# Layer norms in an attention part: statistics by batch-norm instructions on VectorE, normalising on ScalarE

## What is computed

```python
def _layernorm(x, axis=-1, eps=1e-05):
    m = jnp.mean(x, axis=axis, keepdims=True)
    v = jnp.var(x, axis=axis, keepdims=True)
    return (x - m) / jnp.sqrt(v + eps)
...
h = _L0_tok_ref(x, ...)                      # the tower
h = h + _L0_attn_ref(_layernorm(h), W_Q, W_K, W_V)
h = h + _L0_ffn_ref(_layernorm(h), ...)      # top 6 of 64 experts, softmax, projection, own norm
```

## Time and profile before

| what | us |
|---|---|
| median of the runs | 1521.6 |
| the profiled execution | 1521.73 |
| its span in the trace | 1520.0 |
| TensorE busy | 1371.7 |
| VectorE busy | 1183.7 |
| ScalarE busy | 532.2 |
| the attention part up to the experts | 1254 to 1344 |
| the experts and the last norms | 1344 to 1520 |

### The profile page before, as it was taken

How to read it: one execution, slowest core, us unless ns; L and a number is a source line. 1 busy time by engine, 2 the same in 40 slices (tenths; PEclk the granted TensorE clock), 3 DMA queues, 4 the chain that set the end, 5 groups by cost and what they waited for, 6 DMA issues and landing times. The chain is left out here.

```text
span 1520.0 us, 68982 instructions
## 1 busy us (share of the span) xinstructions
PE 1371.7 (90%) x32216; PEld 699.5 (46%) x32216; DVE 1183.7 (78%) x1451; ACT 532.2 (35%) x673; POOL 92.4 (6%) x45
## 2 busy tenths in 40 slices
PE   9889989998899999989999998888789999889996
PEld 3444444445444444454444445555531128843332
DVE  3489999997999999879999997665511118967886
ACT  2522222222222222132222223343379994511211
POOL 1000000000000000000000000000000000045551
PEclk9999999999999999999999999999999999989998
DMA  6233343336766666566666664688844521065420
GB/s 232 90 142 141 131 152 120 135 131 212 277 243 254 246 251 249 195 241 250 257 244 256 243 257 148 252 326 318 342 175 159 181 70 60 8 151 134 118 77 15
DMA packets 55614, 284.35 MB, mean 187 GB/s; under 512 B 16224, under 2 KB 18208, under 8 KB 25504
## 3 DMA queue, kind: packets, MB, share of 16 engines
q1 hardware_dynamic: 34352, 162.22, 32.0%
q10 hardware_dynamic: 21104, 119.76, 19.3%
HBM read 160.33 MB, written 121.63 MB: 186 GB/s over the span
## 5 line engine op out<-in xcount | busy, mean ns | idle before, releaser
L951 ACT ACTIVATE act_c<-slots,conv_b 128x1024 f32<-128x1024 f32 x234 | 258.7, 1115 | 657.4 <-PE slots L603 657.2
L826 DVE STREAM_TRANSPOSE inv_out<-slots 128x1024 f32<-128x1024 f32 x256 | 304.8, 1229 | 77.3 <-PE slots L565 77.3
L603 PEld LDWEIGHTS slots<-inv_w,inv_out 64*64 64x64 f32 x16384 | 268.7, 135 | 194.8 <-issue 184.4
L603 PE MATMUL slots<-inv_w,inv_out 64*64 64x64 f32 x16384 | 299.3, 223 | 14.5 <-issue 8.8
L802 DVE STREAM_TRANSPOSE turned_h<-slots 128x1024 f32<-128x1024 f32 x200 | 237.6, 1227 | 23.7 <-PE slots L498 23.6
L498 PE MATMUL slots<-turned_w,fwd_w 32*64 32x512 f32 x3200 | 204.8, 608 | 22.5 <-DVE inv_out L826 17.2
L777 DVE STREAM_TRANSPOSE turned_w<-act_c 128x1024 f32<-128x1024 f32 x186 | 219.7, 1223 | 0.0
L565 PE MATMUL slots<-turned_k,inv_h 64*64 64x320 f32 x2048 | 167.1, 439 | 36.4 <-DVE turned_h L802 24.4
L587 PE MATMUL slots<-xin,conv_w 32*32 32x512 f32 x3072 | 112.8, 604 | 29.3 <-DMA xin<-act_scratch 15.0
L510 PE MATMUL slots<-turned_h,fwd_h 64*64 64x320 f32 x1600 | 132.8, 443 | 2.1 <-DVE turned_h L802 1.3
L565 PEld LDWEIGHTS slots<-turned_k,inv_h 64*64 64x64 f32 x2048 | 68.1, 132 | 116.3 <-DVE turned_h L802 71.5
(11 more groups left out here) (179 smaller groups left out, 1173.8 us busy)
## 6 DMA issues: line engine op xcount, KB each, us to landing
act_scratch<-act_c ACTq DMA_DIRECT2D x113, 1024.0 KB, 4.1
xin<-act_scratch SPq DMA_DIRECT2D x96, 1024.0 KB, 4.9
act_c<-act_scratch SPq DMA_DIRECT2D x17, 1024.0 KB, 4.9
mode_w<-in_sw_dram SPq DMA_DIRECT2D x20, 640.0 KB, 4.6
at_turned<-level_scratch SPq DMA_DIRECT2D x24, 256.0 KB, 4.1
at_ret_t<-level_scratch SPq DMA_DIRECT2D x20, 256.0 KB, 4.2
xin<-in_x_dram SPq DMA_DIRECT2D x4, 1024.0 KB, 8.6
turned_w<-in_x_turned_dram SPq DMA_DIRECT2D x3, 1024.0 KB, 4.9
```

The lines of the kernel that those rows point to most:

```text
L603: mm = nc.tensor.matmul(banks[half * 64:(half + 1) * 64, 2 * two + odd, at:at + 64], inv_out[rows, t % 2, i, two, s, 2 * half:2 * half + 2 ...
L826: nc.vector.transpose(dst, src).then_inc(inv_turned, 1)
L951: nc.scalar.activation(home[:, :, at, :].rearrange("p i q m -> p q i m"), banks[:, at, :].rearrange("p q (i m) -> p q i m", i=2), ACT.Gelu ...
```

## The change

The norm of x for chunk 3 and all four norms of y are made in another way. Chunks 0 to 2 of x, and the norm of the result at the end, stay.

- `measure_last_x` and `measure_y` replace `centre_x(3)` and `centre_y`, at the same places of VectorE's list. `moments` takes 8 batch-norm statistics (one of each tile of 64 columns), 8 aggregations of them, and one instruction of 8 columns which makes a quarter of variance plus eps.
- `root` on ScalarE stays, on a quarter of the value.
- `scale_last_x` and `scale_y` replace `norm_x(3)` and `norm_y` on VectorE: `scale_and_shift` has five instructions of 8 columns, which give per tile a scale (the inverse root) and a shift (minus mean times the inverse root). The multiplication over 512 columns is gone from VectorE.
- `norm_last_x` and a new `norm_y` on ScalarE make the normalised tiles straight from h, with one activation per tile (8 for a chunk) that takes its scale and its shift from SBUF, one value per partition. For y each reads 64 columns and writes 128, both copies. `double_y` is gone.
- `norm_last_x` stands ahead of `move_x(3)` in ScalarE's list, and `norm_y(0)` behind it, where `double_y(0)` stood ahead. `norm_y(1)` to `norm_y(3)` stand where `double_y` stood.
- `y_turn` waits for `y_set` alone, which ScalarE now raises. `measure_y` of chunks 2 and 3 waits also for `norm_y` of the chunk two earlier, since the statistics lie in two buffers.

```diff
+def moments(nc, link, parts, src, stats):
+
+    for t in range(CT):
+        last = nc.vector.bn_stats(out=parts[:, t, :], in_=src[:, t, :])
+    link(last)
+    for t in range(CT):
+        last = nc.vector.bn_aggr(out=pairs_of(stats)[:, t, :], in_=parts[:, t, :])
+    link(last)
+    return nc.vector.tensor_scalar(stats[:, 1, :], pairs_of(stats)[:, :, 1], EPS, 0.25, ALU.add, ALU.mult)
+
+
+def pairs_of(stats):
+
+    return stats[:, 3:5, :].rearrange("p a t -> p (a t)").rearrange("p (t a) -> p t a", a=2)
+
+
+def scale_and_shift(nc, link, stats):
+
+    link(nc.vector.reciprocal(stats[:, 0, :], stats[:, 2, :]))
+    link(nc.vector.tensor_tensor(stats[:, 0, :], stats[:, 0, :], stats[:, 1, :], ALU.mult))
+    link(nc.vector.tensor_tensor(stats[:, 0, :], stats[:, 0, :], stats[:, 2, :], ALU.add))
+    link(nc.vector.reciprocal(stats[:, 2, :], stats[:, 0, :]))
+    return nc.vector.scalar_tensor_tensor(stats[:, 5, :], pairs_of(stats)[:, :, 0], -1.0, stats[:, 2, :],
+                                          ALU.mult, ALU.mult)
...
                 pe.wait_ge(y_set, c + 1)
-                pe.wait_ge(y_copied, c + 1)
                 turn(s, 128, lambda j: flat(y2[:, c * CT + j, :, :]))
...
-            def centre_x(c):
-
-                dve.wait_ge(h_in[c], 32)
-                centre(nc, link, h[:, tiles_of(c)], centred_x[:, c], squares[:, 0],
-                       stats_x[:, c]).then_inc(x_variance, 1)
...
+            def measure_last_x():
+
+                c = CHUNKS - 1
+                dve.wait_ge(h_in[c], 32)
+                moments(nc, link, parts, h[:, tiles_of(c)], stats_last).then_inc(x_variance, 1)
+
+            def scale_last_x():
+
+                dve.wait_ge(x_root, CHUNKS)
+                scale_and_shift(nc, link, stats_last).then_inc(x_scaled, 1)
...
-            def centre_y(c):
+            def measure_y(c):
 
                 wait_moved("attend", c)
-                centre(nc, link, h[:, tiles_of(c)], centred_y[:, c % 2], squares[:, 1],
-                       stats_y[:, c % 2]).then_inc(y_variance, 1)
-
-            def norm_y(c):
+                if c >= 2:
+                    dve.wait_ge(y_set, c - 1)
+                moments(nc, link, parts, h[:, tiles_of(c)], stats_y[:, c % 2]).then_inc(y_variance, 1)
+
+            def scale_y(c):
 
                 dve.wait_ge(y_root, c + 1)
-                invert_root(nc, link, stats_y[:, c % 2])
-                nc.vector.tensor_tensor(y2[:, tiles_of(c), 0, :], centred_y[:, c % 2],
-                                        along(stats_y[:, c % 2, 2], D), ALU.mult).then_inc(y_set, 1)
+                scale_and_shift(nc, link, stats_y[:, c % 2]).then_inc(y_scaled, 1)
...
             rotate(1, 1)
-            centre_x(3)
+            measure_last_x()
             decay_scores(0)
-            norm_x(3)
+            scale_last_x()
             add_heads(0)
-            centre_y(0)
+            measure_y(0)
             decay_scores(1)
-            norm_y(0)
+            scale_y(0)
             cross(2)
             rotate(2, 0)
             add_heads(1)
-            centre_y(1)
+            measure_y(1)
...
-            norm_y(1)
+            scale_y(1)
             decay_scores(3)
-            centre_y(2)
+            measure_y(2)
             add_heads(3)
-            centre_y(3)
-            norm_y(2)
+            measure_y(3)
+            scale_y(2)
             rank(1)
             take(1)
-            norm_y(3)
+            scale_y(3)
...
-            def double_y(c):
-
-                act.wait_ge(y_set, c + 1)
-                nc.scalar.copy(y2[:, tiles_of(c), 1, :], y2[:, tiles_of(c), 0, :]).then_inc(y_copied, 1)
+            def norm_last_x():
+
+                c = CHUNKS - 1
+                act.wait_ge(x_scaled, 1)
+                for t in range(CT):
+                    last = nc.scalar.activation(normed[:, c, t, :], h[:, c * CT + t, :], ACT.Identity,
+                                                scale=stats_last[:, 2, t:t + 1], bias=stats_last[:, 5, t:t + 1])
+                last.then_inc(normed_set, 1)
+
+            def norm_y(c):
+
+                act.wait_ge(y_scaled, c + 1)
+                for t in range(CT):
+                    last = nc.scalar.activation(y2[:, c * CT + t, :, :], across(h[:, c * CT + t, :], 2), ACT.Identity,
+                                                scale=stats_y[:, c % 2, 2, t:t + 1],
+                                                bias=stats_y[:, c % 2, 5, t:t + 1])
+                last.then_inc(y_set, 1)
...
             root_y(0)
             move_qkv(2, 1)
-            double_y(0)
+            norm_last_x()
             move_x(3)
+            norm_y(0)
             move_y(0)
...
-            double_y(1)
+            norm_y(1)
             move_y(1)
             root_y(2)
             move_gate(1)
             root_y(3)
-            double_y(2)
+            norm_y(2)
             move_y(2)
             exponent(1)
             move_gate(2)
-            double_y(3)
+            norm_y(3)
             move_y(3)
```

More of the change, by code:

```diff
@@ L1082, in transformer @@
         squares = sb("at_squares", [128, 3, CT, D])
-        stats_y = sb("at_stats_y", [128, 2, 3, CT])
+        stats_y = sb("at_stats_y", [128, 2, 6, CT])
+        stats_last = sb("at_stats_last", [128, 6, CT])
+        parts = sb("at_parts", [128, CT, 6])
         normed_t = sb("at_normed_t", [D, 2, SLOT])
@@ L1132, in transformer @@
         y_set = sem("ex_y_set")
-        y_copied = sem("ex_y_copied")
+        x_scaled = sem("at_x_scaled")
+        y_scaled = sem("ex_y_scaled")
         shifted = sem("ex_shifted")
@@ L1681, in root_x @@
                 act.wait_ge(x_variance, c + 1)
-                root(nc, stats_x[:, c]).then_inc(x_root, 1)
+                root(nc, stats_x[:, c] if c < CHUNKS - 1 else stats_last).then_inc(x_root, 1)
             def move_x(c):
```

## The result

The changed kernel takes 1530.4 us (median of 6 runs, 1527.97 to 1535.93); the kernel before, run beside it, takes 1522.38. The ratio is 1.0064 (95% interval 1.004 to 1.0088): the changed kernel is slower, by a little, and the interval leaves out 1. In a second comparison, with more runs of the kernel before, the ratio was 1.0103 (1.008 to 1.0126).

What follows compares the result with a forecast made beforehand. VectorE looked busiest, but late ScalarE norms would delay TensorE's transposes: 7.0 us of waiting plus 1.7 of clock make 8.7, giving 1530.4 from the profiled 1521.73, or 1530.3 against the median. Range: 1526.0 to 1533.0 us.

Steps and rivals of the forecast that it cites:

- 7.0 of waiting: Attention part: late norms on ScalarE delay y's transposes, and from softmax(2) on everything runs 7.0 us later.
- 1.7 of clock: Behind TensorE's wait ahead of y_turn(0): half clock for 3.4 us costs 1.7 us, bounds 0 and about 2.5.
- The walk: Step-by-step delays through the attention part: y_turn(0) 4.8 us late, cross(3) 3.5, y_turn(3) 8.0, the end 7.0.
- chain of waits around 1290 us: Attention part, 10 us from 1290: VectorE busy 9.55 us, the chain nearly VectorE alone, favouring taking work off it.
- VectorE's saving: Five norms in the attention part: 2.0 us saved per chunk, 10 us in all.
- ScalarE's prices: Activations with scale and shift from SBUF: 426 and 480 ns each; norm_last_x 2.8 us, norm_y 3.2 us.
- Rival (b): At y_turn(3): a second clock fall costs up to 1.5 us, with slower aggregations 0.3 more: 1532; chance 0.25.
- (a): ScalarE's activations: both operands fetched together, 334 ns; end 3.1 us late, 1524.7, or 1526.4 with clock fall; chance 0.13.
- (c): Attention part: no fall of the clock at all, 1528.6 us; chance 0.07.
- (d): At cross(3): VectorE's own list releases it, so all ten us saved reach the end, 1511.6; chance 0.02.
- (e): At measure_y(3): its new wait for norm_y(1) could bind, but costs nothing over the walk; no chance given.

Runs made afterwards that it cites:

- filled_waits: The changed kernel with dummy matmuls put into TensorE's waits ahead of x_turn(3) and y_turn(0) to y_turn(3): 1526.51 us, ratio 1.004 to the kernel before.
- fill_first: The changed kernel with dummy matmuls only ahead of x_turn(3) and y_turn(0): 1526.28 us, ratio 1.0044 to the kernel before.
- late_old: The changed kernel with y chunks 1 to 3 normalised the old way, x chunk 3 and y chunk 0 the new way: 1527.63 us, ratio 1.0058.
- one_operand: The changed kernel with activations taking only the scale from SBUF (shift left out) and dummies in TensorE's waits: 1520.43 us, ratio 1.0011 to before.

## Why the prediction was right, and where it was not

The sum was 7.0 of waiting and 1.7 of clock, thus 8.7; 8.0 was measured beside it. The walk was right and the clock was not: its term was 1.7 us and measured 6.9 to 9.6. That the total still fits the first comparison is luck, as the points below on the clock and on the profile of before show.

**The chain of before.** The prediction says that the chain of waits around 1290 us consists nearly of VectorE alone. It doesn't. From 1284.17 to 1294.25 it runs over TensorE and ScalarE (start and length, kernel before):

```profile
1286.17 0.89 PE slots L1228 x8
...
1287.08 1.02 ACT at_normed_t L1677
...
1288.23 1.54 PE slots L1249 x8
1289.77 1.02 PE slots L1228 x8
1290.79 1.49 PE slots L1249 x8
1292.28 1.97 PE slots L1292 x16
```

This is `x_turn(3)`, its move, and the list behind `y_turn(0)`, the very place into which the change put ScalarE's two rows of eight; VectorE has the chain again from 1294.28 to 1327. So the question with which the prediction begins, who sets the pace, had a different answer at the place that mattered. The sum doesn't suffer, since its walk goes through this place all the same.

**VectorE's saving.** Eight statistics take 1.11 us (forecast 1.10) and eight aggregations 0.64 (0.7). The saving of 10 us is there, 8.5 of it as busy time, and none of it reaches the end.

**ScalarE's prices.** 428 and 484 ns (forecast 426 and 480), rows of eight in 2.76 and 3.19 us (2.8 and 3.2). The rule of the Trainium skill for pointer operands, "ScalarE: Activation LUTs", section "What ACT_TABLE_LOAD costs", is borne out with 89 to 91 ns for the second one. The rule on small tiles, of the Trainium skill's page "VectorE: DVE Perf Modes", section "The TRN2 errata — SBUF-src ops pay a fixed extra latency per instruction", points the same way: `double_y` was one instruction of 619 ns, and `norm_y` is eight in 3.19 us. They differ in columns and operands, though, so this is no measure of the fixed cost.

**The walk.** It can be read without the clock in filled_waits. `y_turn(0)` is at 36.60 behind the tower's end, forecast 1291.7 - 1254.9 = 36.8. `cross(3)` is 3.76 later than before (3.5), `y_turn(1)` 4.8 (4.6), `y_turn(2)` 5.5 (5.5), `y_turn(3)` 8.0 (8.0), `softmax(2)` 6.9 (7.1), `softmax(3)` 6.93 (7.0).

**The clock, the term that was mis-sized.** "Half the clock for 3.4 us costs 1.7 us of work", with 2.5 as its upper end. It lasted 17.1 to 20.5 us and cost 6.3 to 6.9 us in three profiles. The step that failed is taking a length from the earlier trace rows for a fall in another place. The prediction also counted only the work ahead of `cross(3)`; TensorE's list sets the time behind it as well. And the step from the long wait to the fall holds in its outcome only, since in two of the three profiles the clock fell behind the 1.48 us wait already. Rival (b), the second fall, came in 2 of 3 profiles, with 1.6 and 2.9 us where I had said up to 1.5. One of these falls had the tower's length, 3.4 us; the other lasted 6.8.

**The profile of before, an assumption that wasn't stated.** The sum was made against one execution in which the attention part had no fall. Three later ones had one, of 5.2 us, which is absent in the changed kernel's profiles: there the fall comes 7 to 9 us later, at the waits. By profiles alone, from the tower's end to the span's end, the changed kernel takes 278.4 us (mean of three) and before 267.8 (mean of four): 10.6 us. Against the profile without a fall it is 13.2. The timed comparisons gave 9.7 and 15.7, with about 3.5 to either side, 12.7 in the mean. So the likely size of the change is 10 to 13 us, over the 8.7 forecast, and the closeness of 1530.3 to 1530.4 is luck: the median of the second comparison, 1534.1, lies above the range given.

Two things say which of the two sizes to believe. In the table the last column agrees within 1.7 us with the difference to 265.1 in all seven edited kernels, and lies 2.2 to 4.3 us above the difference to 267.8. And the mean granted clock over the whole execution is on record for the timed runs too: 0.9895 for 68 runs of before, 0.9892 for 22 of filled_waits and fill_first, and 0.9834 for 12 of the changed kernel. Multiplied by the span, 1 minus this mean tells how much clock was lost. The changed kernel lost 0.0061 x 1526 = 9.3 us more than before in these runs. In the profiles, from the tower's end on, it lost 20.0 us (mean of three), before 10.6 without the fall and 14.5 with it: 9.4 more, or 5.5. filled_waits and fill_first lost 10.3 and 10.6 us there, as before did without its fall, and their timed runs have its mean clock. So by this estimate, which takes the tower's losses as equal on average, the timed executions of before mostly had no fall, and the upper end, some 13 us, is the better figure. Why the profiles of before show the fall so much more often stays open.

**The tower.** It ended between 1248.0 and 1262.3 us in kernels whose tower is the same, 1248.0 to 1254.9 in the four profiles of before alone. Two spans therefore say little on a change of 8 us; the offsets from the tower's end agree within 0.1 us in the three profiles of before that have the fall.

**The other rivals.** (a) falls by 428 ns. (c), no fall, didn't come in the changed kernel; its price is seen in filled_waits, 7.0 expected and 6.93 in the profile. (d) falls by the 11.86 us that VectorE waits ahead of `cross(3)`. (e) was seen as foreseen: `measure_y(3)` waits 0.24 us, and nothing follows from it. By the chances given the range leaves out 0.12 (half of (a), (d) and the unseen), not 0.15.

## What to carry to other kernels

Work moved from a busy engine to one with room still costs if it lands on the road between two others: ask at each place what the follower waits for, not which engine is fuller. A wait put on TensorE is to be priced with the clock behind it, over all the work that follows at half speed, and filled with dummy matmuls if it can't be avoided. A length of such a fall, read at one place of a kernel, is not the length at another. Before one profile carries a sum, ask whether another execution of the same kernel would show the same clock; and compare stretches from a common event, not from the start of the span.

## What the runs showed of the hardware

- The granted clock stayed at half for 17.1 to 20.5 us around two waits of TensorE, of 1.48 and 4.28 us with 1.03 us of work between, in 4 of 4 profiles (the changed kernel's and late_old's). In three of them it fell ahead of the longer wait. In the first profile of the changed kernel it stayed low though TensorE was busy for 13.84 of the last 13.90 us. Behind a wait of 2.06 us in the tower it was 3.4 us.
- A wait of 2.84 us ahead of `y_turn(3)` had a fall with it in 3 of 5 profiles, of 3.4, 3.4 and 6.8 us.
- The clock also fell without such a wait, in 3 of 4 profiles of the kernel before, for 13.7 us. The page "TensorE: Matmul & The Clock Gate", section "A second HAM failure mode: psum-queue depth-cycling", of the Trainium skill tells of a clock that swings with many short idle times between groups of matmuls. The 0.47 to 0.59 us here may be such, but the same ones stand in the profile that didn't fall, so the trace doesn't decide it.
- Dummy matmuls in the two waits (12 and 36, or 6 and 24 in one_operand) kept the clock at its full level there in 3 of 3 profiles.
- An operand from SBUF seems to cost VectorE time too: 64 columns with two of them take 310 ns, and a statistic of 64 columns 212. The two instructions differ in more than the operands, so the price of one isn't shown.
- In a row of eight, batch-norm statistics of 64 columns start every 0.13 us (212 ns for one, 1.11 us in all), and an aggregation of 6 values takes 153 ns, eight of them 0.64 us.
